# Order of tiles 0 to 2 and tile 3 between a cross-attention and a mixture of experts, and of the last two head groups' outputs

## The reference

```python
x = x + xattn(layernorm(x), ctx, mask)   # 16 heads of 32, 1601 keys in each of 8 batches, masked softmax
n = layernorm(x); q = n @ W_q.T          # the self block: no softmax
x = x + (q @ n.T) @ n                    # within a batch of 64 tokens
n = layernorm(x)                         # 8 experts, the best 2 of each token
logits = n @ gate_w + gate_b             # softmax over the two best
x = x + sum_e cw[:, e] * (relu(n @ w1[e] + b1[e]) @ w2[e] + b2[e])   # 512 -> 2048 -> 512
```

## Time and profile before

| | us |
|---|---|
| median of 3 runs | 1293.33 (1292.92 to 1294.27) |
| the profiled execution | 1289.2 |
| its span, first to last instruction | 1287.5 |
| PE busy | 1246.4 (97%) |
| DVE busy | 842.4 (65%) |
| ACT busy | 675.0 (52%) |
| POOL busy | 159.2 (12%) |
| mean granted clock of PE | 0.988 of full |

### The profile page before, as it was taken

One profiled execution on the slowest core, in us unless ns is written; L12 is line 12 of the kernel. 1 busy time (PEld: TensorE's weight loads), 2 busy tenths in 40 slices (PEclk: granted clock), 3 DMA queues, 4 the chain that ended last, 5 costly groups with the idle time before them and its releaser, 6 DMA issues.

```text
span 1287.5 us, 22172 instructions
## 1 busy us (share of the span) xinstructions
PE 1246.4 (97%) x8497; PEld 1161.5 (90%) x8497; DVE 842.4 (65%) x2186; ACT 675.0 (52%) x1193; POOL 159.2 (12%) x86
## 2 busy tenths in 40 slices
PE   7999999999999999999999999999878999999997
PEld 6799999999999999999999999988767988989996
DVE  4556656566565666556566566685576788877877
ACT  5345545535544553464455455354444676767673
POOL 2203101300400220040031013000021000000012
PEclk9999999999999999999999999999969999999999
DMA  9002200310220040022022003100226667677763
GB/s 329 27 1 88 82 1 1 118 52 1 91 79 2 27 142 1 1 91 79 2 90 80 1 7 143 38 2 7 97 74 241 226 240 254 238 240 250 230 220 114
DMA packets 61506, 129.04 MB, mean 100 GB/s; under 512 B 3572, under 2 KB 21120, under 8 KB 61160
## 3 DMA queue, kind: packets, MB, share of 16 engines
q1 hardware_dynamic: 59240, 120.85, 27.4%
q0 software_dynamic: 2176, 6.95, 1.6%
HBM read 121.89 MB, written 15.34 MB: 107 GB/s over the span
## 4 chain that ended last, share of the span: by engine, by line
PE 92%; DVE 4%; ACT 2%; DMA 1%; issue 1%; POOL 0%; SPq 0%; POOLq 0%; DVEq 0%
PE ptp L830 24%; PE work L830 20%; PE work L1128 8%; PE pv L975 7%; PE ptp L959 7%; PE work L868 6%; PE work L1130 4%; PE ptp L1149 2%; PE ptp L1152 2%; PE ptp L1151 2%; PE ptp L1153 2%; PE ptp L1150 2%; PE work L837 2%; PE ptp L837 1%; DVE pt L1379 1%; DMA raw<-in_ctxT 1%
## 5 line engine op out<-in xcount | busy, mean ns | idle before, releaser
L830 PE MATMUL ptp<-vw_hi,cx_hi 128*128 128x256 f32 x832 | 241.8, 291 | 0.0
L830 PE MATMUL ptp<-vw_lo,cx_hi 128*128 128x256 f32 x832 | 235.4, 283 | 0.0
L830 PE MATMUL ptp<-vw_hi,cx_lo 128*128 128x256 f32 x832 | 235.4, 283 | 0.0
L518 POOL TENSOR_TENSOR cx_lo<-raw,cx_hi 128x1664 fp32r<-128x1664 f32 x30 | 113.8, 3792 | 666.3 <-ACT cx_hi L578 666.3
L830 PE MATMUL work<-cx_hi,kw_hi 128*128 128x400 f32 (+1 forms) x504 | 175.5, 348 | 2.9 <-POOL cx_lo L518 1.7
L830 PEld LDWEIGHTS ptp<-vw_hi,cx_hi 128*128 128x128 f32 x832 | 159.3, 191 | 17.0 <-issue 17.0
L830 PE MATMUL work<-cx_hi,kw_lo 128*128 128x400 f32 (+1 forms) x504 | 173.6, 345 | 0.0
L830 PE MATMUL work<-cx_lo,kw_hi 128*128 128x400 f32 (+1 forms) x504 | 173.2, 344 | 0.0
L1379 DVE TENSOR_TENSOR pt<-ptp,pt 128x512 fp32r<-128x512 f32 (+1 forms) x224 | 141.3, 650 | 33.3 <-ACT pt L578 29.8
L830 PEld LDWEIGHTS ptp<-vw_lo,cx_hi 128*128 128x128 f32 x832 | 159.3, 191 | 0.0
L830 PEld LDWEIGHTS ptp<-vw_hi,cx_lo 128*128 128x128 f32 x832 | 159.3, 191 | 0.0
(11 more groups left out here) (268 smaller groups left out, 2384.9 us busy)
## 6 DMA issues: line engine op xcount, KB each, us to landing
w1raw<-in_w SPq DMA_DIRECT2D x32, 1024.0 KB, 5.1
w2raw<-in_w SPq DMA_DIRECT2D x32, 1024.0 KB, 6.9
raw<-in_ctxT SPq DMA_DIRECT2D x31, 832.0 KB, 6.3
pr<-in_mask SPq DMA_DIRECT2D x8, 800.5 KB, 4.4
xrow<-x_rows SPq DMA_DIRECT2D x7, 256.0 KB, 6.2
y_rows<-y_out_rows POOLq DMA_DIRECT2D x7, 256.0 KB, 2.4
xin<-in_x SPq DMA_DIRECT2D x1, 1024.0 KB, 8.9
qwraw<-in_qwT SPq DMA_DIRECT2D x1, 1024.0 KB, 11.1
```

What stands on the lines that cost most here:

```text
L518: pool.tensor_tensor(cx[1][:, :, sl], raw[:, k % 2], cx[0][:, :, sl].bitcast(F32), ALU.subtract).then_inc(c_lo, 1)
L830: last = pe.matmul(dst, lhs(i, c), rhs(j, c), start=(c == 0 and (i, j) == (0, 0)), stop=(c == n - 1 and (i, j) == (1, 0)))
```

## The change

In the list of the last batch the query step goes behind the transposing steps. DVE makes tile 3's row weights at the query step, and both last groups' outputs after the last low part. In the self block tiles 0 to 2 go through scores, values, additions, layer norm, transposition and logits in front of tile 3's; the second layer norm is two calls; banks and the two lists follow. ACT waits for the end of the attention, and makes w1's first high part, in front of the query copies. DVE's low parts of w2 move behind the choice, and its copies of places and weights, now `places_and_weights`, into the first expert.

```diff
--- before.py
+++ after.py
@@ -66,7 +66,7 @@
         steps += s[0] + v[0:2] + s[1] + e[0:1] + v[2:3] + e[1:2] + v[3:4] + s[2] + v[4:6] + s[3]
         if h and last:
             turned, queried = [("n", 0, j) for j in range(EARLY)], [("q", 0, m) for m in range(EARLY_Q)]
-            steps += v[6:] + e[2:] + turned + queried + t + w[:1] + w[1:]
+            steps += v[6:] + e[2:] + turned + t + queried + w
             continue
         steps += e[2:3] + v[6:] + e[3:]
         if last:
@@ -100,8 +100,8 @@
 
 
 
-FILLED = (["q0_1", "att3", "b1", "q0_2", "q0_3", "pre0", "pre1", "turn0_3", "pre2", "q1", "own0", "pre3", "own1", "own3",
-           "own2", "turn1_0", "turn1_1", "turn1_2", "turn1_3", "logits", "earlier", "total", "places", "weights",
+FILLED = (["q0_1", "att3", "b1", "q0_2", "q0_3", "turn0_3", "pre0", "pre1", "pre2", "own0", "own1", "own2", "q1", "pre3",
+           "own3", "turn1_0", "turn1_1", "turn1_2", "turn1_3", "logits", "earlier", "total", "places", "weights",
            "b2_0", "b2_1", "b2_2", "b2_3"])
 COPIED = [n for n in FILLED if n[:4] == "turn" or n[0] == "q" or n == "b1"]
 
@@ -355,7 +355,7 @@
         stored = sem("output_stored")
 
         yb = ptp + [pv]
-        turn_banks = [yb[2], work[2], yb[0], yb[1]]
+        turn_banks = [work[1], work[2], yb[2], work[3]]
 
         def sum_bank(last, g):
 
@@ -662,6 +662,8 @@
             def fold(b, last, g):
 
                 act.wait_ge(pt_used, NPT * b + TPH * (g + 1) + PTD)
+                if last and g == 3:
+                    act.wait_ge(pv_free, 4 * b + g + 1)
                 sums = sum_bank(last, g)
                 act.activation(folded[0:2 * HD, :], sums[2 * HD:P, 0:2 * P], ACT.Copy)
                 act.activation(folded[2 * HD:P, :], sums[0:2 * HD, 2 * P:4 * P], ACT.Copy).then_inc(folded_done, 1)
@@ -706,10 +708,6 @@
                     act.wait_ge(p2_used, NP * n + p - 1)
                 copy(w2s[0][:, s], w2raw[:, s], w2_hi)
 
-            def first_weights(p):
-                w1_part(0, 0, p, True)
-                w2_part(0, 0, p, True)
-
             def turned(k, t, bank):
 
                 act.wait_ge(m_full, filled(f"turn{k}_{t}"))
@@ -720,25 +718,34 @@
                 act.wait_ge(m_full, filled(f"q0_{m_}"))
                 copy(gT[:, m_, MINE], work[m_ - 1][:, MINE], m_out)
 
+            def tokens_hi(t):
+
+                act.wait_ge(ln2, TT + t + 1)
+                copy(xn[0][:, t], hn[:, t], x_hi)
+
+            act.wait_ge(att_over, 4)
+            w1_part(0, 0, 0, True)
             early_query(1)
             act.wait_ge(m_full, filled("b1"))
             copy(b1T[:], pv[:, 0:P], m_out)
             root(3, range(EARLY, TT))
             for m_ in range(2, C):
                 early_query(m_)
-            act.wait_ge(att_over, 4)
             turned(0, EARLY, yb[1])
-            w1_part(0, 0, 0, True)
+            w2_part(0, 0, 0, True)
+            w1_part(0, 0, 1, True)
+            root(4, range(EARLY))
             act.wait_ge(m_full, filled("q1"))
-            copy(gT[:, :, EARLY * P:T], yb[2][:].rearrange("p (c n) -> p c n", c=C), m_out)
-            w2_part(0, 0, 0, True)
-            root(4, range(TT))
-            for t in range(TT):
+            copy(gT[:, :, EARLY * P:T], work[3][:].rearrange("p (c n) -> p c n", c=C), m_out)
+            for t in range(EARLY):
+                tokens_hi(t)
+            for t in range(EARLY):
+                if t == EARLY - 1:
+                    root(5, range(EARLY, TT))
                 turned(1, t, turn_banks[t])
-            for t in range(TT):
-                act.wait_ge(ln2, TT + t + 1)
-                copy(xn[0][:, t], hn[:, t], x_hi)
-            first_weights(1)
+            turned(1, EARLY, turn_banks[EARLY])
+            tokens_hi(EARLY)
+            w2_part(0, 0, 1, True)
 
             def gathered(n):
 
@@ -1025,30 +1032,31 @@
             pe.transpose(pv[:, 0:P], b1r[:], ident[:]).then_inc(m_full, 1)
             for m_ in range(2, C):
                 early_query(m_, work[m_ - 1]).then_inc(m_full, 1)
-            pe.wait_ge(m_out, copied("q0_3"))
-            self_scores(0, work[0])
-            self_scores(1, work[1])
             pe.wait_ge(ln2, TT)
             turn_tile(EARLY, yb[1]).then_inc(m_full, 1)
-            self_scores(2, work[2])
+            pe.wait_ge(m_out, copied("q0_3"))
+            for t in range(EARLY):
+                self_scores(t, work[t])
+            self_values(0, yb[0])
+            self_values(1, yb[3])
+            self_values(2, yb[2])
             pe.wait_ge(m_out, copied("turn0_3"))
             for m_ in range(C):
-                last = plain(yb[2][:, m_ * P:(m_ + 1) * P], lambda c: wq2[:, c, m_ * P:(m_ + 1) * P],
+                last = plain(work[3][:, m_ * P:(m_ + 1) * P], lambda c: wq2[:, c, m_ * P:(m_ + 1) * P],
                              lambda c: hT[:, c, EARLY * P:T])
             last.then_inc(m_full, 1)
-            self_values(0, yb[0])
             pe.wait_ge(m_out, copied("q1"))
-            self_scores(3, yb[1])
-            self_values(1, yb[3])
-            self_values(3, work[1])
-            self_values(2, work[0])
-            for t in range(TT):
+            self_scores(EARLY, yb[1])
+            self_values(EARLY, yb[1])
+            for t in range(EARLY):
                 pe.wait_ge(ln2, TT + t + 1)
                 turn_tile(t, turn_banks[t]).then_inc(m_full, 1)
             pe.wait_ge(ld2[2], 16)
-            for t in range(TT):
-                last = logits(t)
-            last.then_inc(m_full, 1)
+            for t in range(EARLY):
+                logits(t)
+            pe.wait_ge(ln2, TT + EARLY + 1)
+            turn_tile(EARLY, turn_banks[EARLY]).then_inc(m_full, 1)
+            logits(EARLY).then_inc(m_full, 1)
             pe.wait_ge(zeroed, 7)
             pe.wait_ge(chosen_done, 1)
             for t in range(TT):
@@ -1401,9 +1409,10 @@
                     kind, a, j = step
                     for i in turns(step):
                         pt_item(b, i)
-                    if kind == "w":
-                        if last and a == 2:
-                            row_weights(range(EARLY, TT))
+                    if kind == "w" and not (last and a == 2):
+                        if last and a == 3:
+                            group_out(b, last, 2)
+                            dve.wait_ge(att_rows, 4 * b + 3)
                         group_out(b, last, a)
                     if kind == "a" and j == 0:
                         dve.wait_ge(att_rows, 4 * EARLY_B)
@@ -1411,6 +1420,8 @@
                         row_weights(range(EARLY))
                     if kind == "l":
                         layer_norm(xs, hn, ln2, 2, range(EARLY))
+                    if kind == "q":
+                        row_weights(range(EARLY, TT))
                     if kind in "vskanq":
                         item(b, last, step)
 
@@ -1472,17 +1483,17 @@
                     r = slice(S * a, S * (a + 1))
                     dve.tensor_copy(pre[r, t, r], bank[r, r]).then_inc(pre_done, 1)
 
+            w1_part(0, 0)
             dve.wait_ge(zeroed, 7)
             for t in range(EARLY):
                 blocks(t, work[t])
-            w1_part(0, 0)
             add(0, yb[0])
+            add(1, yb[3])
+            add(2, yb[2])
+            layer_norm(xs, hn, ln2, 4, range(EARLY))
             blocks(EARLY, yb[1])
-            add(1, yb[3])
-            add(3, work[1])
-            add(2, work[0])
-            layer_norm(xs, hn, ln2, 4)
-            w2_part(0, 0)
+            add(EARLY, yb[1])
+            layer_norm(xs, hn, ln2, 5, range(EARLY, TT))
 
             dve.wait_ge(ld2[3], 16)
             dve.wait_ge(m_full, filled("logits"))
@@ -1572,6 +1583,27 @@
                     dve.wait_ge(m_full, filled(f"b2_{t}"))
                     dve.tensor_tensor(xs[:, t], xs[:, t], yb[t][:], ALU.add).then_inc(y_out, 1)
 
+            def places_and_weights():
+
+                dve.wait_ge(m_full, filled("places"))
+                step(dve.tensor_copy(placeT[:], yb[2][0:E, :]))
+                dve.wait_ge(m_full, filled("weights"))
+                dve.tensor_copy(cwT[:], yb[3][0:E, :]).then_inc(cwT_done, 1)
+                chosen_e = idxf[:, :, 0:2].rearrange("p t k -> p k t")
+                step(dve.scalar_tensor_tensor(out=slot_f[:], in0=chosen_e, scalar=-float(CAP), in1=row_f[:],
+                                              op0=ALU.mult, op1=ALU.add))
+                step(dve.tensor_scalar(ours[:], chosen_e, float(LASTE), None, ALU.is_lt))
+                join()
+                step(dve.scalar_tensor_tensor(out=ours[:], in0=slot_f[:], scalar=float(SLOTS), in1=ours[:],
+                                              op0=ALU.is_lt, op1=ALU.mult))
+                step(dve.scalar_tensor_tensor(out=y_f[:], in0=chosen_e, scalar=float(SLOTS), in1=slot_f[:],
+                                              op0=ALU.mult, op1=ALU.add))
+                join()
```

(28 more changed lines are left out.)

## The result

| | before | after |
|---|---|---|
| median, us | 1293.12 (4 runs) | 1276.72 (4 runs, 1274.77 to 1280.6) |
| ratio after / before | | 0.9878 (95%: 0.9862 to 0.9893) |
| the profiled execution | 1289.2 | 1274.77 |
| its span | 1287.5 | 1273.0 |
| mean granted clock | 0.988 | 0.993 |

A forecast was written before the change was run, and what follows sets the result against it. PE bounds the kernel, busy 97%, except in the stretch from 900 to 975 us. There 11.4 - 2.4 - 0.6 + 2.2 = 10.6 us gained, from 1293.3 to 1282.7; range 1278.0 to 1287.5.

The forecast's parts named there:

- Part 1, the tail: Attention's end: transposes fill the wait before the query product, outputs follow the last low part; attention ready 4.1 us earlier.
- Part 2, the self block: Self block: tiles 0 to 2's transposes and logits run under DVE's work on tile 3; 11.4 us earlier, including the tail's 4.1.
- The clock, 2.4: Self block from 935.4: thin PE work may fall to half clock, costing 0 to 4.9 us; middle, 2.4, deducted.
- POOL, 0.6: Tile 3's second normalisation: POOL's low parts slow DVE in one meeting, 0.6 us deducted; bounds nothing and 2.4.
- The gather: After the logits: the gather stays at half clock as before; 1.85 us gained as the upper bound.
- Part 3, the first expert, 2.2: Before the first expert's second pass: PE's idle 2.20 goes, gaining 2.2 us; costs bounded by nothing and 2.29.
- rival 3: Self block: logits of tiles 0 to 2 don't get hidden; only tile 3's normalisation comes 5.1 earlier; 1288.2; 4%.
- 1: Self block: thin work halves the clock from 935 on and POOL meets DVE each time; gain 6.3, 1287.0; 8%.
- 4: Gather and hidden passes: PE stays at half clock into the first expert, making the kernel slower, 1295.7; 4%.
- 2: First expert: DVE's w2 piece lands on the path and gives the part back; gain 6.1, 1287.2; 4%.
- best case: Whole stretch: no clock fall, no POOL meeting, gather at full clock; gain 15.5, 1277.8.
- Queues: Load queues: SP's load of the third w1 piece (935.48) goes some 10 us earlier; nothing waits longer.

The follow-up runs named there:

- after_third: The changed kernel, unchanged, profiled a third time: 1275.93 us.
- w2_only: Kernel before with only w2's low parts moved behind the choice and into the first expert's second pass, copies of places and weights left: 1290.36 us, ratio 0.9968.
- before_third: The kernel before, unchanged, profiled a third time: 1293.88 us.
- before_fourth: The kernel before, unchanged, profiled a fourth time: 1294.81 us.
- query_only: Kernel before with only the two transposing steps put ahead of the query step: 1289.73 us, ratio 0.9970.

## Why the prediction was wrong

**Part 1, the tail: right, and small.** Values ended at 913.97 (914.15 forecast) and the attention at 916.80 (917.4); the transposes of tile 3's rows came 4.3 us earlier than before, counted from the query's start, against 4.1. But in two of three later profiles of before the half clock behind the stand lasts longer, and the tail is 24.3; undone, it costs 4.8. **Part 2, the self block:** the steps came as listed: tile 3 normalised from 921.40, tiles 0 to 2 done at 934.9 (935.9), tile 3 at 940.1 (941.1), logits done at 943.49, which is what the sum gave *without* its two deductions (943.8). **The clock, 2.4: mis-sized.** It fell only for tile 3's eight products, 1.84 us instead of some 1.0, 0.8. I had taken the middle between never and at once; the clock was full through nearly all of the work that I called thin. **POOL, 0.6: nothing in the normalisation.** The small instructions of tile 3's layer norm keep 0.15 to 0.18 us each. Where POOL does cost is one cast in three profiles of four *before*, 0.8 to 1.0, and the change took nearly all of that away, as POOL's first three instructions are done by 938.5 and the fourth before the last logit (in after_third just behind it, and the cast takes 0.32); the one meeting that I charged was one to credit. The Trainium skill (SBUF — State Buffer, "Who interferes with whom") has a cast in a two-port mode wait for the whole of POOL's instruction. The trace agrees: each long cast ends 0.03 to 0.08 us behind the end of the instruction of POOL that ran when it came, so its price is what is left of POOL's 1.24, and not the 0.59 that I took from the row of small casts; in which mode these casts ran, no trace shows. **The gather** was at half, as taken. **The net of the block was luck.** On the first profile the deductions were 2.7 us too many. In the later ones the block gives 4.1, and 0.9 more in *choice*, close to the net 4.3 of the forecast; but only because the logits of the kernel before, which I had read at half to their end, are at full for most of their length there. Two errors met.

**Part 3, the first expert, 2.2: the step that failed.** "PE's idle 2.20 goes: 2.2 us" was read in the one execution of four in which DVE's copy began at once and the clock stayed up behind the stand. What makes the copy late, POOL's scatters, was in none of my steps: I had followed POOL's queue for what it waits for and not for whom it holds up. In three other profiles the same kernel stands 3.77 to 4.14 us there and runs the second pass at half: *pass* and *second* together are 6.6 longer than after the change on average (4.2 and 2.3), against 2.4 in the first. The runs by their medians give less, undone 4.3, alone 4.4, its larger half alone 6.0 (3.9 to 8.0 by its interval): some two to three times the 2.2. In the tail I had priced the clock behind an idle time of 2.32; behind one of 2.20 I had not.

**The carry-over, unstated as a risk.** Against its own execution the forecast was 1278.6 and 1274.77 came; of these 3.8, 3.2 lie in the segments (2.7 in *self*, 0.2 each in *tail* and *pass*) and the rest outside, which varies so without any change. Then I subtracted the same 10.6 from the median, which was 4.1 above the profile. Those 4.1 were not spread over 1289 us: by the three later profiles they are the longer stands, the half clock behind them and the late cast, less 3.0 for the faster logits, all in just the stretch that the change clears. So the difference to the median was itself mostly gain: 17.2 by the later profiles against 13.8.

**Rivals.** None of the four came (and rival 3's 1288.2 had left out the 2.2 of part 3, which its condition doesn't touch). 1 and 4 wanted more half clock; 2 wanted DVE's w2 piece on the path, and the second pass began with no wait; 3 is refuted by the logits under tile 3's normalisation. What was missing was a rival on the fast side with a place: stands that are longer in most executions than in the profiled one. Even the best case, 1277.8, had no such term. **Queues:** SP's load of w1's third piece went at 924.17 instead of 935.48, and from 900 us on neither PE nor ACT nor DVE waited for a load.

## What to carry to other kernels

If the profiled execution is faster than all the others, profile again before pricing a stand: here the median's extra time sat where PE stood, and removing the stands gave that too. Price an idle time of PE such as these 2.2 us as a range, from itself alone to itself plus, from the rows at either level, the half clock behind it, in every place and not only where it shows; and price half-clock work that a change removes as a range too, for here it was partly at full in most profiles. And look at what POOL has in flight beside a copy of DVE on the path.

## What the runs showed of the hardware

The clock behind the same stand is not fixed: after 2.20 to 2.34 us of idle the next products were at full in the first profile's second pass (4.70 us) and partly at half in w2_only's (6.33), and in the tail, behind 2.32 to 2.34 us, it fell in the first four products (before_third), later (before, before_fourth) or, in query_only, not at all. In the changed kernel 24 products of 8 columns, 2.82 us, were at full.

A POOL scatter that starts under DVE's subtraction of two SBUF tiles is stretched. POOL, then DVE, changed kernel:

```profile
954.60 0.96 POOL L559 DMA_INDIRECT x_rows<-hn,row_i  x1 [0.30 <-issue]
955.86 2.52 POOL L559 DMA_INDIRECT x_rows<-hn,row_i  x1 [0.30 <-issue]
```

```profile
955.26 2.28 DVE L1469 TENSOR_TENSOR w_lo<-w2raw,w_hi 128x2048 fp32r<-128x2048 f32 x1
```

It ends (958.38) 0.84 us after that subtraction does (957.54). So it is in all nine profiles with the low part there: one scatter takes 2.43 to 3.04 us and ends 0.83 or 0.84 after the subtraction; where the part was left ahead none of the last six is over 0.97. The Trainium skill (SBUF — State Buffer, "Who interferes with whom") infers that a subtraction of two tiles leaves the writing of descriptors alone. These rows don't decide that, since a scatter here also reads its row numbers (`row_i`) from SBUF; they show that the scatter as a whole is not left alone. Nothing here waited for the scatter. In the other direction, a DVE copy from PE's bank starts up to 1.26 us after POOL's last scatter has ended, in seven profiles 1.4 to 2.1 behind what it waits for, and the profile names no releaser that fits.
